# One-hot rows of chosen keys and of places: built by VectorE instead of GpSimd

## What is computed

```python
qp = LN(x) @ Wq.T                                   # [512, 256] for each batch
idx = argmax(qp @ ctx.T, axis=-1)                   # one key number (0..511) for each query
mem = ctx[idx]                                      # keys may be chosen many times
mk, mv = split(mem @ Wkv.T)                         # 16 channels each
x = x + tanh(g0) * (softmax(heads(qp) @ mk.T / 4) @ mv) @ Wc.T
x = x + tanh(g1) * top2_of_8_experts(LN(x))         # gelu(x @ w1 + b1) @ w2 + b2
```

## Time and profile before

| | |
|---|---|
| median of 3 runs | 1070.39 us (1065.84 to 1070.52) |
| profiled execution, its own time | 1074.56 us |
| its span in the trace | 1072.8 us |
| mean granted TensorE clock | 0.90 |
| TensorE matmul busy | 874.6 us, 82% |
| VectorE busy | 545.8 us, 51% |
| GpSimd busy | 455.1 us, 42% |
| ScalarE busy | 406.8 us, 38% |

### The profile page before, as it was taken

The page is one execution under the profiler, slowest core; times in us unless marked ns, Lnnn a source line. Parts: engine busy times, 40 slices in busy tenths (PEclk is TensorE's granted clock), DMA queues, the critical chain, the costliest instruction groups (busy, mean ns, idle before and its releaser), DMA issues. The chain is left out here.

```text
span 1072.8 us, 20727 instructions
## 1 busy us (share of the span) xinstructions
PE 874.6 (82%) x6428; PEld 608.4 (57%) x6429; DVE 545.8 (51%) x1517; ACT 406.8 (38%) x802; POOL 455.1 (42%) x492
## 2 busy tenths in 40 slices
PE   2486989798888889788732049999999999999995
PEld 1232435354444444333221038999898998989894
DVE  2467576757676767663302224454545444454542
ACT  1220364635454554566611023333434333333331
POOL 5847263656565564335253002242323333232323
PEclk9776899998999999998755569999999999999998
DMA  4533324242523424222321142222222323231310
GB/s 138 128 94 92 71 73 86 82 100 80 125 82 105 93 73 90 66 96 96 103 77 49 62 122 50 41 45 44 42 46 41 56 39 58 39 57 33 55 18 1
DMA packets 65691, 76.39 MB, mean 71 GB/s; under 512 B 7392, under 2 KB 59360, under 8 KB 65504
## 3 DMA queue, kind: packets, MB, share of 16 engines
q1 hardware_dynamic: 51328, 58.74, 21.1%
q0 software_dynamic: 14304, 16.93, 9.1%
HBM read 47.68 MB, written 29.53 MB: 72 GB/s over the span
## 5 line engine op out<-in xcount | busy, mean ns | idle before, releaser
L595 ACT ACTIVATE prob<-ps_a 128x512 f32<-128x512 f32 x256 | 150.5, 601 | 207.5 <-PE ps_a L988 201.8
L724 DVE TENSOR_REDUCE row_max<-ps_d 128x2 f32<-128x512 f32 x256 | 170.3, 683 | 82.8 <-PE ps_d L967 71.4
L2276 PE MATMUL ps_h<-x_hi,w_split 128*128 128x256 bf16 x1248 | 212.3, 274 | 0.0
L2290 PE MATMUL ps_y<-w_split,hidden 128*128 x1248 | 206.4, 273 | 0.0
L2276 PE MATMUL ps_h<-x_lo,w_split 128*128 128x256 bf16 x624 | 170.8, 274 | 0.0
L2290 PE MATMUL ps_y<-w_split,h_lo 128*128 x624 | 170.1, 273 | 0.0
L2159 ACT ACTIVATE hidden<-ps_h,bias 128x256 f32<-128x256 f32 x312 | 131.0, 471 | 88.2 <-PE ps_h L2276 88.1
L2133 POOL DMA_INDIRECT out<-y,token_at x78 | 127.5, 1635 | 43.9 <-POOL token_at L2131 30.5
L967 PE MATMUL ps_d<-k_st,w_split 96*128 96x256 bf16 x512 | 107.0, 296 | 35.6 <-DVE row_max L724 25.2
L2276 PEld LDWEIGHTS ps_h<-x_hi,w_split 128*128 x1248 | 122.7, 98 | 14.4 <-issue 0.2
L2290 PEld LDWEIGHTS ps_y<-w_split,hidden 128*128 128x128 bf16 x1248 | 122.1, 98 | 14.1
(11 more groups left out here) (184 smaller groups left out, 1113.8 us busy)
## 6 DMA issues: line engine op xcount, KB each, us to landing
w_stage<-w SPq DMA_DIRECT2D x32, 512.0 KB, 3.9
xg<-queue SPq DMA_DIRECT2D x39, 260.0 KB
w_split<-q_split SPq DMA_DIRECT2D x24, 256.0 KB, 6.4
x_in<-x SPq DMA_DIRECT2D x8, 512.0 KB
ctx_sb<-ctx_t SPq DMA_DIRECT2D x8, 512.0 KB, 3.8
x<-x SPq DMA_DIRECT2D x8, 512.0 KB, 3.9
q_split<-q_hl SPq DMA_DIRECT2D x16, 256.0 KB, 2.5
out<-x SPq DMA_DIRECT2D x8, 512.0 KB, 3.1
```

The costliest lines, as they stand in the source:

```text
L595: a.activation(prob[n % 2][:, j, :], ps_a[step % 2][:], ACT.Exp, scale=SCALE).then_inc(exp_ready, 1)
L724: v.tensor_reduce(row_max[:, t, 2 * pair:2 * pair + 2], bank.rearrange("p (h r) -> p h r", h=2), AX.X, ALU.max).then_inc(max_taken, 1)
L2276: last = t_.matmul(ps_h[n][:, c, :], k.w1_split[:, bass.ds(e, 1), part, kt, f].rearrange("p a f -> p (a f)"), xs[s][:, kt, :], start=(q == ...
L2290: last = t_.matmul(ps_y[s][:, t, :], hs[s][:, f, token], k.w2_split[:, bass.ds(e, 1), part, f, :].rearrange("p a d -> p (a d)"), start=(q ...
```

## The change

`chosen_keys` and `places` are taken out of GpSimd's program. VectorE issues the same instructions itself: after each index search it waits for it, copies the index to `best` and compares; after the scan of `positions` it makes the four comparisons. GpSimd keeps `values`, which now raises a semaphore of its own, `values_ready`, and `pack` waits for that beside `place_ready`. Before a search VectorE no longer waits for GpSimd's `chosen_ready` of the batch before, but for `packed`.

```diff
-            def chosen_keys(s, t):                       # on GpSimd, steps 7, 9, 11, 13
-                pool.wait_ge(scores_read, LT * s + t + 1)
-                if s:
-                    pool.wait_ge(counts_ready, s)
-                chain.then(g.tensor_copy(best[:, t:t + 1], top8_at[:, t, 0:1]))
-                g.tensor_scalar(chosen[:, t, :], column[:], best[:, t:t + 1], None, ALU.is_equal).then_inc(chosen_ready, 1)
...
-                chain.step(g.tensor_tensor(value_cols[:, :, V1:2 * V1], value_f[:], value_cols[:, :, 0:V1], ALU.subtract))
-
-            def places(s):                               # on GpSimd, step 20
-                pool.wait_ge(position_ready, s + 1)
-                chain.settle()
-                for t in range(LT):
-                    last = g.tensor_scalar(place[:, t, :], column[:, 0:SLOTS], position[:, t:t + 1], None, ALU.is_equal)
-                last.then_inc(place_ready, 1)
+                g.tensor_tensor(value_cols[:, :, V1:2 * V1], value_f[:], value_cols[:, :, 0:V1],
+                                ALU.subtract).then_inc(values_ready, 1)
...
             def best_key(s, t, bank):
                 dve.wait_ge(scores_ready, LT * s + t + 1)
                 if s:
-                    dve.wait_ge(chosen_ready, LT * (s - 1) + t + 1)
+                    dve.wait_ge(packed, s)
                 chain.then(v.max(top8[:, t, :], bank))
                 v.max_index(top8_at[:, t, :], top8[:, t, :], bank).then_inc(scores_read, 1)
+                dve.wait_ge(scores_read, LT * s + t + 1)
+                chain.then(v.tensor_copy(best[:, t:t + 1], top8_at[:, t, 0:1]))
+                v.tensor_scalar(chosen[:, t, :], column[:], best[:, t:t + 1], None, ALU.is_equal).then_inc(chosen_ready, 1)
...
-                    dve.wait_ge(place_ready, s)
+                    dve.wait_ge(values_ready, s)
...
-                v.tensor_tensor(position[:], position[:], offset[:, 0:LT], ALU.add).then_inc(position_ready, 1)
+                chain.then(v.tensor_tensor(position[:], position[:], offset[:, 0:LT], ALU.add))
+                for t in range(LT):
+                    last = v.tensor_scalar(place[:, t, :], column[:, 0:SLOTS], position[:, t:t + 1], None, ALU.is_equal)
+                last.then_inc(place_ready, 1)
...
             def pack(s):
                 pe.wait_ge(place_ready, s + 1)
+                pe.wait_ge(values_ready, s + 1)
```

More of the change, by code:

```diff
@@ L270, in flow @@
                                                              sem("shift_ready"))
-        position_ready = sem("position_ready")
+        values_ready = sem("values_ready")
         xn_ready, xn_turned, xn_t_ready = sem("xn_ready"), sem("xn_turned"), sem("xn_t_ready")
@@ L308, in flow @@
         DVE_SPLIT_MAX, DVE_COPY_MAX, DVE_CHOOSE, DVE_SHARES, DVE_QUEUE = 25, 27, 27, 30, 31
-        POOL_QUERY_LO, POOL_CHOSEN, POOL_VALUES, POOL_PLACE = 6, (7, 9, 11, 13), 18, 20
+        POOL_QUERY_LO, POOL_VALUES = 6, 18
         POOL_DEVIATION, POOL_X_DEVIATION, POOL_X, POOL_SCATTER = 18, 22, (22, 23, 24, 25), 31
@@ L531, in _ @@
                     query_lo(s)
-                for t in due(s, POOL_CHOSEN, step):
-                    chosen_keys(s, t)
                 if step == POOL_DEVIATION and is_batch(e):
@@ L537, in _ @@
                     values(s)
-                if step == POOL_PLACE and is_batch(s):
-                    places(s)
                 if step == POOL_X_DEVIATION and is_batch(p + 3):
```

## The result

The changed kernel takes 1075.15 us (median of 7 runs, 1073.41 to 1078.6) where the kernel before takes 1070.39 in the runs beside them (median of 7, 1065.84 to 1071.1). The ratio is 1.0057, interval [1.0037, 1.0076]: 0.6% slower. Two later comparisons on other chips gave 1.0055 [1.0033, 1.0078] and 1.0077 [1.0053, 1.0101]. The forecast was 1072, the range 1060 to 1082. The two executions that were profiled here stand the other way round, 1073.93 us after and 1074.56 before, so where the loss lies is read from the pairs of profiles further down.

What follows compares the result with a forecast made beforehand. VectorE was taken to set the pace in steady turns where the places stand, and chains of waits in turns -2 and -1. Terms +3.8, -4.4 and +2.3 gave +1.7 us: 1076.3 profiled, 1072 as median, range 1060 to 1082.

Steps and rivals of the forecast that it cites:

- turn -2: Early pipeline turn, 0 to 105 us: counts 1.6 us earlier, places 2.8 us less, together -4.4 us.
- turn -1: Turn after turn -2: counts 2.9 us late, places add 1.0, the 1.60 wait goes, together +2.3 us.
- the six steady turns: Later turns: VectorE's work makes TensorE 1.8 us later, waits for `place` of 7.0 us go; +3.8 us in all.
- Prices: Moved instructions on VectorE: cast 0.16 us, chosen row 0.40, place row 0.29; four places 1.0 with waits.
- Rival (b): VectorE comparisons run at one element a cycle: +14 us, 1084; chance 0.12.
- Rival (a): VectorE's new work is hidden and the waits for `place` simply go: -10 us, 1060; chance 0.23.
- Rival (c): Turns -2 and -1: a VectorE comparison loses to back-to-back GpSimd instructions, another 2.1 us each, 1076; chance 0.12.
- rival (d): New short stops at the scores lower TensorE's granted clock, about 1.3 us a turn, +8 us, 1080; chance 0.10.
- the pace theory: VectorE's new time ahead of a reduction partly becomes TensorE's wait; chosen rows alone +5.5 us, places alone -4.6.
- GpSimd: Steady turns: its own saving of 10.0 us a turn is worth nothing beyond the ended wait for `place`.

Runs made afterwards that it cites:

- the piece held back: Whole change, but in turns -2 and -1 GpSimd's second weight piece waits for VectorE's third chosen row: 1067.6 us, ratio 1.0093 to the kernel before.
- the chosen rows alone: Kernel before with only casts and chosen comparisons moved to VectorE, ahead of the reduction; places stay on GpSimd: 1073.1 us (ratio 1.0154), on another chip 1085.3 (1.0142).
- the spare comparison: Kernel before plus a cast and comparison on VectorE behind each search, into an unread tile; GpSimd keeps all its work: 1084.03 us, ratio 1.0121.
- the places alone: Kernel before with only the four place comparisons moved to VectorE; chosen rows stay on GpSimd: 1057.9 us (ratio 1.0009), on another chip 1067.42 (0.9974).

## Why the prediction came out as it did

The mechanism and the direction of each step were right, the sum 3 to 6 us too small: +1.7 forecast, +4.8, +6.9 and +8.1 measured. The pair of profiles from one chip (1070.46 and 1074.76 us, +4.3) splits it by the prediction's terms: `pack` of turn -2 comes 2.4 us earlier (forecast 4.4), turn -1 takes 4.9 more (forecast 2.3), the six steady turns 2.0 more (forecast 3.8), and the rest 0.2 less (forecast 0).

- **Prices.** 0.40 for a chosen row, 0.353 measured; 0.16 for the cast, 0.154; 0.29 for a place, 0.286, and four in 0.87 us instead of 1.0. Rival (b), one element a cycle, is out. The Trainium skill, page VectorE: DVE Perf Modes, section on the perf-mode tier table, together with the fixed part of 0.23 us from the earlier trace rows gave an estimate of 0.36 for a chosen row; the trace agrees.
- **Steady turns.** Forecast +0.6 each. In turn 1, at full clock, it is +0.7 (30.99 against 30.25). Later turns at full clock take 30.06 to 30.38 us before, once 31.68, and 30.85 to 30.89 or 32.05 to 32.35 after; the higher figures are turns in which the second score comes 1.2 to 1.5 us later, and they come with both kernels. The six distances hold 334.0 us against 332.0 on the one chip and 335.1 against 334.8 in the first pair, so +2.0 and +0.3 where +3.8 was forecast; where the low clock and the late second score fall decides differences of that size. Rival (a), all hidden, is out: TensorE waits at the scores. The tile of step 19 takes 1.04 of the 1.29 back.
- **Turn -2.** Forecast -4.4, measured -3.4 from the first score to `pack`. The search-by-search count forgot that the weight piece now stands right behind `q_hl` and blocks the cast of the key columns for 1.80 us, so that the searches behind it are late and the fourth score waits 2.09 us. With the piece held back the stretch is 4.7 us shorter than before, so this collision explains the whole miss. Rival (c) had the wrong victim: the comparison won the race, the cast behind it lost. On the one chip the first score also started 1.0 us later, ahead of anything that was moved.
- **Turn -1.** This is the term that was furthest off: +2.3 forecast, +4.1 and +4.9 between the two `pack`s in the two pairs of profiles. The second score waits 1.55 us for its collision instead of 0.13, about as said, and the third and the fourth wait 0.87 instead of 0.28, so 0.6 more where I had 0.45. The third and the fourth score also run partly at the low clock, 3.31 and 2.67 us instead of 1.96 each in the first profile and 3.49 and 3.02 in the second. That is 2.1 and 2.6 us, and without it the turn is 2.1 to 2.2 us longer from the first score to `pack`, close to the +2.3. So the pace was right, and the clock was put at nothing. It is rival (d), which I had for steady turns and not for this one. The second `pack`, forecast at 94.2, comes at 96.92.
- **Where the two halves stand.** The runs showed the part that I did not see: the chosen rows alone cost 15 us, not the 5.5 of the pace theory, and the places give about 7 of it back when they are added to them, not the 4.6 expected of them. That my sum came out near is in part luck: both halves were missed, in opposite directions. At 1.0 to 1.1 us the pace of the chosen rows is 0.2 to 0.3 a turn above my 0.8, and the places give 0.4 a turn where I had 0.2; more low clock (up to 5.5 us) and turn -1 hold the rest.
- **GpSimd.** That its relief is worth nothing in a steady turn was right: with the spare comparison, GpSimd not relieved, turn 1 takes 31.25 us, as with the chosen rows. In turn -2 it is worth 2.2 us.

**Open.** Three things stay open. The first is why the places alone give 2.9 us on one chip and nothing on another; the kernel before was not profiled on that other chip. The second is how many falls of the clock a given stop brings. I can show that the low-clock time differs, behind the last `pack` too, not that one stop causes one fall. The third is the late second score. In the full turns it comes either about 4.4 us (before) or 4.8 us (after) behind the first, or 1.2 to 1.5 us later than that, at full clock too (0.1 to 0.4 later in two profiles on the chip with the low times). In one late turn VectorE starts its search 1.4 us after the score has ended, and in one early turn at once (0.04). On the chip with the low times the places alone and the whole change with the chosen rows behind the reduction are early in every full turn; on the other chips most of the last four turns are late. No run here shows why.

## What to carry to other kernels

When two engines take turns on two buffers, count what stands ahead of the instruction that gives a buffer back, not how busy the engine is: 0.5 us behind each of four searches cost 15 us a run ahead of the reduction, and nothing behind it. A step that comes off an idle engine pays only through the wait that it ends, so look for a place on the new engine where this wait still ends and nothing is queued behind the moved work; here that turned a loss of 0.6 to 0.8% into a gain of 0.9 to 1.3%, of which a part (2.4 of 10.2 and 5.6 of 16.5 us in the profiles) came from a later stretch at a higher granted clock. Where short stops of TensorE are added or taken away, look at the granted clock of every later stretch as well, and test halves before trusting a sum: two profiles of one kernel differ by several us in where the low clock falls.

## What the runs showed of the hardware

- **Exclusion between VectorE and GpSimd.** A VectorE comparison or cast that meets a GpSimd `TENSOR_TENSOR` of 2.1 us ends with that instruction or up to 0.15 us behind it (1.59 and 1.80 us instead of 0.35 and 0.20). With two GpSimd instructions back to back the waiting VectorE instruction was not held by the second one, and the next VectorE one was. The Trainium skill, page SBUF — State Buffer, section Who interferes with whom, states the exclusion; the trace agrees.
- **The clock.** In most of the last four turns with a selection 3.4, 6.8 or 10.2 us are spent at the low level. The amount differs between kernels that differ by 0.5 us on VectorE, and between two executions of one kernel (6.8, 10.2, 3.4 and 3.4 us in one profile of the kernel before, 6.8, 3.4, 6.8 and 6.8 in the other).
- **Chips differ.** The same kernels take 0.9 to 1.3% less on one chip than on another: 1056.7 and 1070.31 (before), 1073.1 and 1085.3 (chosen rows), 1057.9 and 1067.42 (places). Only runs on the same chip can be compared to 0.5%.
